# Two layers of gated cross attention on one core: held contexts, expert biases inside the expert products, gate picks on GpSimd, new orders

## The chip, the cores and the metric

The kernel runs on one NeuronCore of a Trainium2 chip. The metric is the device time in microseconds. Engines are named TensorE (PE in the rows; PEld is its weight load), VectorE (DVE), ScalarE (ACT), GpSimd (POOL) and SyncE (SP, which here only issues DMAs).

## The reference

There are 32 independent batches, each with x of 112 x 256 and a context of 375 x 192, in float32. Four updates follow each other:

```
x = x + tanh(g_xattn[0]) * (softmax(q k^T / 8) v) Wo^T + bo, 4 heads, q from layernorm(x), k and v from the context
x = x + tanh(g_ffn[0])   * layernorm(x) (W + up_aux lora_up lora_down down_aux)^T + b
x = x + tanh(g_xattn[1]) * softmax(q k^T) v             one head of 256, biases on q, k, v
x = x + tanh(g_ffn[1])   * (self attention of 16 heads + experts)
```

(the gate of the first line also covers bo, that of the second b). The experts: a softmax over 8 gate logits, of which the two largest are kept as weights; the output is the sum over e of weight[e] * (x W_experts[e] + b_experts[e]). layernorm has no scale or shift.

## The kernel before, in words

Every engine runs its own written program. The batches go through a software pipeline: in iteration i, each body handles batch a = i (layer 0's keys and values), b = i-1 (layer 0's scores), c = i-2 (layer 0's end, its linear layer and the queries of layer 1), d = i-3 (layer 1's attention, the projections of the last layer) and e = i-4 (16-head attention, experts, store). There are 32 + 4 iterations; the first five and the last four are unrolled, the others are one loop. What an engine does in which order is the list of calls in its `body`; there is no scheduler. Engines meet by semaphores: a `Chain` counts the steps of one batch, and `after(step, batch)` is the value to wait for.

Nearly all products are split: an operand is a float16 high half and a float16 low half, and a product is three matmuls (high x high, high x low, low x high). ScalarE writes the high half (`hi`), VectorE the low half (`lo`).

PSUM is one tile `quad` of four banks and the banks B, C, D and E. `quad` is used in turn by the keys and values (`project_k`, `project_v`), the scores of layer 0 (`scores0`, `scores0_T`) and those of the 16 heads (`scores2`, `scores2_T`). A score product is made twice: once for its row maximum (VectorE reduces it, `max0`, `max1`, `max2`, and TensorE transposes the maximum, `max0_T`, ...), and once transposed, with the maximum subtracted. Bank E holds two experts at a time: `experts(j)` makes 6 matmuls of 512 columns, `weigh_experts(j)` (ScalarE) scales them by the weights cgS into `part`, and `add_experts(j)` (GpSimd) adds them to `acc`.

The experts' bias is a product of its own. VectorE picks the two weights (`gate_pick`, `gate_combine`, `gate_weights`, `gate_scaled`), TensorE transposes them (`combine_T`), VectorE copies them as a high and a low half (`combine_copy`, `combine_lo`), TensorE multiplies them with the biases (`expert_bias`), and VectorE starts the sum with it (`start_sum`: acc = bias + x3). GpSimd's first `add_experts` and TensorE's `max2_T` wait for that sum.

GpSimd also makes the layernorms' 1/deviation (`rstd`, two small operations), which VectorE's `normalise` waits for, and one half of the context (`ctxT_hi`). Layer 1 needs the context's halves two iterations after layer 0: SyncE copies them from `kvA` to `kvB` and from there to `kc0`, `kcA`, `kcB`, `kcm`.

## Time and profile before

| | |
|---|---|
| median of 3 runs | 924.86 us (920.3 to 925.35) |
| the profiled execution | 923.47 us, its span 921.5 us |
| mean granted TensorE clock | 0.977 of full speed |
| busy, share of the span | PE 846.2 us (92%), DVE 785.2 us (85%), ACT 563.2 us (61%), POOL 392.7 us (43%) |
| matmuls | 11764 |
| DMA | 61.82 MB, mean 67 GB/s |

The span runs from the first to the last instruction. Matmuls are pipelined, and the end of one is modelled, so one row's length overlaps the next; the time that a matmul takes from TensorE is the distance from its start to the next start. A mean of a group is of single instructions. `project_k` is the mark by which iterations are told apart here: for batch 17 it starts at 449.76 us, for batch 18 at 476.22 us.

### The profile page before, as it was taken

Reading aid. Unit: us, or ns where it says so; the run is one execution under the profiler, and the core shown is the slowest. Engines: PE = TensorE matmul, PEld = TensorE weight load, DVE = VectorE, ACT = ScalarE, POOL = GpSimd, SP = SyncE. Lnnn points to the kernel's source line nnn. Section 1 sums busy time; section 2 is a strip of 40 time slices with the busy share of each in tenths; the row PEclk is TensorE's granted clock in tenths of the full one; section 3 lists DMA queues with packets and bytes.
Section 4 is the critical chain, followed back from the end, with each engine's and each line's share of the span. In section 5 each row is a group of like instructions: output and inputs, shape, how many; then the busy total and the mean of one; then the engine's idle time right before and its main releaser. Section 6 shows DMA issues by size and latency. Waiting matters only on the chain. (4 is left out here: it accounts for less than half of the span.)

```text
span 921.5 us, 34388 instructions
## 1 busy us (share of the span) xinstructions
PE 846.2 (92%) x11764; PEld 666.0 (72%) x11764; DVE 785.2 (85%) x1910; ACT 563.2 (61%) x1230; POOL 392.7 (43%) x603
## 2 busy tenths in 40 slices
PE   4678999999999999999999999999999999999876
PEld 2467777778777777787777778777777787777654
DVE  3588989989998989899899998998999889888654
ACT  2444666666666666666666666666666666666443
POOL 3311545433455453344554433445544334454433
PEclk9789999999999999999999999999999999999987
DMA  7311222121112211212222122122221211111100
GB/s 257 114 61 57 66 79 66 59 73 61 58 61 75 75 62 62 68 57 63 64 75 74 52 73 63 53 70 66 75 70 54 75 60 56 61 59 56 39 6 6
DMA packets 41285, 61.82 MB, mean 67 GB/s; under 512 B 6158, under 2 KB 28036, under 8 KB 41128
## 3 DMA queue, kind: packets, MB, share of 16 engines
q1 hardware_dynamic: 41256, 61.43, 20.9%
q8 instruction: 18, 0.29, 0.1%
q14 instruction: 11, 0.09, 0.0%
HBM read 37.77 MB, written 3.67 MB: 45 GB/s over the span
## 5 line engine op out<-in xcount | busy, mean ns | idle before, releaser
L1317 POOL TENSOR_TENSOR acc<-part,acc 112x256 f32<-112x256 f32 x256 | 212.4, 830 | 298.9 <-DVE acc L1163 275.3
L820 ACT ACTIVATE part<-bankE,cgS 112x256 f32<-112x256 f32 x256 | 107.2, 473 | 3.0 <-PE bankE L329 2.3
L1266 POOL TENSOR_SCALAR ln_ve<-ln_mv 112x1 f32<-112x1 f32 x128 | 33.9, 265 | 174.5 <-DVE ln_mv L967 173.2
L329 PE MATMUL bankE<-wexs_hi,xT_hi 128*112 128x512 f16 x256 | 99.3, 388 | 3.4 <-ACT part L820 3.4
L1270 POOL TENSOR_TENSOR ln_rs<-ln_ve,cst 112x1 f32<-112x1 f32 x128 | 94.5, 738 | 10.7
L329 PE MATMUL bankE<-wexs_hi,xT_lo 128*112 128x512 f16 x256 | 97.7, 382 | 0.0
L329 PE MATMUL bankE<-wexs_lo,xT_hi 128*112 128x512 f16 x256 | 97.7, 382 | 0.0
L1067 DVE TENSOR_TENSOR p_lo<-p2T,p_hi 112x896 f16<-112x896 f32 x64 | 67.6, 1094 | 9.6 <-ACT p_hi L811 9.6
L1130 DVE TENSOR_REDUCE mx<-quad 112x8 f32<-112x896 f32 x64 | 69.6, 1088 | 1.0
L740 ACT ACTIVATE p0T<-quad 125x896 f32<-125x896 f32 x64 | 46.2, 722 | 38.6 <-PE quad L445 38.6
L973 DVE TENSOR_SCALAR xn<-x,ln_mv,ln_rs 112x256 f32<-112x256 f32 x96 | 54.9, 572 | 5.9 <-POOL ln_rs L1270 2.0
L803 ACT ACTIVATE p2T<-quad 112x896 f32<-112x896 f32 x64 | 55.2, 914 | 5.9 <-PE quad L579 2.7
L1001 DVE TENSOR_TENSOR p_lo<-p0T,p_hi 125x896 f16<-125x896 f32 x64 | 54.1, 845 | 5.1 <-ACT p_hi L748 5.1
L811 ACT ACTIVATE p_hi<-p2T 112x896 f16<-112x896 f32 x64 | 57.0, 944 | 0.0
L988 DVE TENSOR_REDUCE mx<-quad 112x2 f32<-112x750 f32 x64 | 56.7, 925 | 0.3 <-PE quad L423 0.2
L329 PE MATMUL quad<-kvA,linw_hi 128*128 128x375 f16 x192 | 53.2, 333 | 2.7 <-ACT p0T L740 1.5
L329 PE MATMUL quad<-linw_hi,kvA 128*125 128x256 f16 x288 | 54.8, 274 | 0.0
L748 ACT ACTIVATE p_hi<-p0T 125x896 f16<-125x896 f32 x64 | 48.9, 764 | 4.6
L956 DVE SCALAR_TENSOR_TENSOR kvA<-ctf,kvA 128x375 f16<-128x375 f32 x32 | 33.0, 1030 | 20.4 <-POOL kvA L1308 20.4
L329 PEld LDWEIGHTS bankE<-wexs_hi,xT_lo 128*112 128x112 f16 x256 | 33.5, 131 | 22.4 <-issue 0.6
L329 PE MATMUL bankC<-p1T,ctn 125*128 125x112 f32 x384 | 48.1, 275 | 0.4 <-ACT p1T L767 0.4
L329 PEld LDWEIGHTS bankE<-wexs_hi,xT_hi 128*112 128x112 f16 x256 | 33.4, 131 | 20.8 <-ACT part L820 4.5
(239 smaller groups left out, 3275.5 us busy)
## 6 DMA issues: line engine op xcount, KB each, us to landing
ctf<-in_ctx_T SPq DMA_DIRECT2D x32, 375.0 KB, 3.1
ctn<-in_ctx_n SPq DMA_DIRECT2D x32, 375.0 KB
kvB<-kvA SPq DMA_DIRECT2D x32, 281.2 KB, 2.4
kc<-kvB SPq DMA_DIRECT2D x32, 187.5 KB
xin<-in_x SPq DMA_DIRECT2D x32, 112.0 KB, 2.0
x<-in_x SPq DMA_DIRECT2D x32, 112.0 KB, 2.1
out_x<-xout SPq DMA_DIRECT2D x32, 112.0 KB, 1.9
wex<-in_w_exp SPq DMA_DIRECT2D x1, 2048.0 KB, 9.9
```

The costliest lines, as they stand in the source:

```text
L329: last = mm(o, w, m, start=(n == 0), stop=(n == len(terms) - 1))
L748: act.activation(p0_hi[:, :, cs, :, 0:LQ].rearrange("p r c j q -> p r (c j) q"), p0T[:, :, cs].rearrange("p r c j q -> p r (c j) q"), ACT. ...
L803: act.activation(p2T[:, 2 * g:2 * g + 2].rearrange("p n i q -> p n (i q)"), quad[0:LQ, 2 * g:2 * g + 2, 0:4 * LQ], ACT.Exp, scale=HD1 ** - ...
L811: act.activation(p2_hi[:, 2 * g:2 * g + 2, :, 0:LQ], p2T[:, 2 * g:2 * g + 2], ACT.Copy).then_inc(st2[g].sem, 1)
L820: act.activation(part[:, e, :], bankE[0:LQ, n * D:(n + 1) * D], ACT.Identity, scale=cgS[:, e:e + 1])\
L973: ts(xn[n][:], src[:], ln_mv[n][:, 0:1], ln_rs[n][:], ALU.subtract, ALU.mult).then_inc(ln[n].sem, 1)
L988: dve.tensor_reduce(mx0[:].rearrange("p (r j) -> p r j", r=2)[:, :, g], quad[0:LQ, 2 * g:2 * g + 2, 0:LK], AX.X, ALU.max).then_inc(sh0[g]. ...
L1001: tt(p0_lo[:, :, cs, :, 0:LQ].rearrange("p r c j q -> p r (c j) q"), p0T[:, :, cs].rearrange("p r c j q -> p r (c j) q"), p0_hi[:, :, cs, ...
L1067: tt(p2_lo[:, 2 * g:2 * g + 2, :, 0:LQ].rearrange("p n i q -> p (n i) q"), p2T[:, 2 * g:2 * g + 2].rearrange("p n i q -> p (n i) q"), p2_h ...
L1130: dve.tensor_reduce(mx2[:].rearrange("p (n w) -> p n w", n=4)[:, 2 * g:2 * g + 2, 0:4], quad[0:LQ, 2 * g:2 * g + 2, 0:4 * LQ].rearrange("p ...
L1270: pool.tensor_tensor(ln_rs[n][:], ln_ve[n][:], minus_half, ALU.pow).then_inc(ln[n].sem, 1)
L1317: pool.tensor_tensor(acc[:], part[:, 2 * j + n, :], acc[:], ALU.add).then_inc(moe_sum[j].sem, 1)
```

## The change

- **Contexts.** `kvB` is gone. SyncE writes `kvA` to a DRAM tensor `hold` of 32 slots (`hold_context`) and loads the layer-1 tiles from there (`fetch_held`); the wait of `copy_A_to_B` for the previous copy out of `kvB` is gone.
- **Biases.** Each `experts(j)` gets a seventh matmul of 512 columns, 16 (in two rows, a high and a low half) times the biases of its two experts. `combine_T`, `expert_bias`, `combine_copy`, `combine_lo`, `start_sum` and `acc` go. The biases are packed once, by ScalarE (`bex_half`) and VectorE (`bias_experts(j)`).
- **Picks.** `gate_pick`, `gate_combine` and `gate_weights` run on GpSimd, the last one writes cgS directly (the gate's scale is in `ths`); `gate_scaled` goes. The reciprocal stays on VectorE (`gate_recip`).
- **Sums.** `add_experts` adds in `part` itself: expert k's slot becomes the sum of 0..k and x3. `finish` reads the last slot, in a sixth stage f, one iteration later; `weigh_experts` waits slot by slot.
- **Loads.** The weights of `lin` come in four DMAs, the constants, the keys' start values and the LoRA matrices in another order; the high halves of WK and WV are separate.
- **Orders.** All bodies have a new order, and loops start at another place of the iteration. Six iterations are unrolled ahead, five behind.

```
-STAGES = 5
+STAGES = 6
-PEEL = 5
+PEEL = 6
-        kvA, kvB = sb("kvA", [P, 3, LK], F16), sb("kvB", [P, 3, LK], F16)
+        kvA = sb("kvA", [P, 3, LK], F16)
+        hold = nc.dram_tensor("hold", [NB, P, 3, LK], F16, kind="Internal").ap()
...
-            def copy_B_to_C(b):
+            def fetch_held(b):
-                sp.wait_ge(copyAB.sem, copyAB.after("c", b))
+                sp.wait_ge(held.sem, held.after("c", b))
                 if past(b - 1):
                     sp.wait_ge(st1.sem, st1.after("ps", b - 1))
-                sp.dma_start(kc0[:], kvB[:, 0:2, :]).then_inc(copyBC.sem, DMA)
+                sp.dma_start(kc0[:], hold[b, :, 0:2, :]).then_inc(fetched.sem, DMA)
...
-            def copy_A_to_B(a):
+            def hold_context(a):
                 sp.wait_ge(ctT[0].sem, ctT[0].after("lo", a))
                 sp.wait_ge(ctT[1].sem, ctT[1].after("lo", a))
-                if past(a - 1):
-                    sp.wait_ge(copyBC.sem, copyBC.after("m", a - 1))
-                sp.dma_start(kvB[:], kvA[:]).then_inc(copyAB.sem, DMA)
+                sp.dma_start(hold[a], kvA[:]).then_inc(held.sem, DMA)
...
             def max2_T(d):
                 pe.wait_ge(sh2.sem, sh2.after("max_b", d))
-                pe.wait_ge(acc_s.sem, acc_s.after("sum", d))
+                pe.wait_ge(qk_s.sem, qk_s.after("klo", d))
...
             def experts(j, d):
-                    wex_lo[:, c, cols].rearrange("p e n -> p (e n)"))]).then_inc(moe[j].sem, 1)
+                    wex_lo[:, c, cols].rearrange("p e n -> p (e n)"))]
+                    + [(ones16, bex[:, 2 * j * D:2 * (j + 1) * D])]).then_inc(moe[j].sem, 1)
...
+            def gate_pick(d):
+                pool.wait_ge(gate_s.sem, gate_s.after("indexf", d))
...
+                pool.tensor_scalar(pick0[:], iota, topf[:, 0:1], top[:, 0:1], ALU.is_equal, ALU.mult).then_inc(gate_s.sem, 1)
+                pool.tensor_scalar(pick1[:], iota, topf[:, 1:2], top[:, 1:2], ALU.is_equal, ALU.mult).then_inc(gate_s.sem, 1)
...
+            def gate_weights(d):
+                pool.wait_ge(gate_s.sem, gate_s.after("comb", d))
+                pool.wait_ge(rs_s.sem, rs_s.after("recip", d))
...
+                pool.tensor_scalar(cgS[:], comb[:], rsg[:], ths[0:LQ, 0:1], ALU.mult, ALU.mult).then_inc(gate_s.sem, 1)
...
-                    pool.tensor_tensor(acc[:], part[:, 2 * j + n, :], acc[:], ALU.add).then_inc(moe_sum[j].sem, 1)
+                    k = 2 * j + n
+                    pool.tensor_tensor(part[:, k, :], part[:, k, :], part[:, k - 1, :] if k else x3[:], ALU.add).then_inc(moe_sum[j].sem, 1)
...
+            load_ctx_T(0)
+            sp.dma_start(lin[:, WK], w_lin[:, WK]).then_inc(wk_in, DMA)
             sp.dma_start(gate_in[:], gates).then_inc(gates_in, DMA)
-            load_ctx_T(0)
-            sp.dma_start(lin[:, WK:WV + 1], w_lin[:, WK:WV + 1]).then_inc(kv_in, DMA)
+            sp.dma_start(lin[:, WV], w_lin[:, WV]).then_inc(wv_in, DMA)
+            load_x(0)
...
                 if A: project_k(a)
                 if DD: norm_T(3, d, bankD, pv2, "norm", d - 1)
+                if A: project_v(a)
                 if C: norm_T(2, c, bankC, f0_s, "x2", c)
-                if A: project_v(a)
                 if DD: project_vg(d)
...
                 if EE: exp2(0, e)
-                if EE: exp2(1, e)
                 if B: hi(qs, "ps", b, q_hi[:], cols(bankB, KD, LQ), 1 / SW, st0[1], "ps", b - 1)
+                if EE: exp2(1, e)
```

The last two pieces are lines of TensorE's and of ScalarE's `body`.

Three places of the new orders, in the loop. First TensorE around the sums of layer 1 (bankC<-p1T,ctn is `sums1`; cgb holds the weights to be transposed, bex16 the biases). Before:

```order
L329 MATMUL bankB<-stack,c16 112x256
L609 ISA
L610 REGISTER_ALU
L611 MATMUL bankD<-cst,cgb 128x112
L510 ISA
L329 MATMUL bankC<-p1T,ctn 128x112 x6
L616 ISA
L617 MATMUL bankD<-bex16,cT 112x256
L329 MATMUL bankE<-wexs_hi,xT3_hi 112x512
L329 MATMUL bankE<-wexs_lo,xT3_hi 112x512
```

Now:

```order
L333 MATMUL bankC<-m1h,kcm 125x112
L553 ISA
L555 ISA
L565 MATMUL quad<-k2_hi,q2_hi 112x112 x16
L402 ISA
L404 ISA
L406 MATMUL bankB<-cst,xn0 128x112 x2
L516 ISA
L333 MATMUL bankC<-p1T,ctn 128x112 x6
L596 ISA
```

The transpose of the weights and the bias product are gone; `scores2` and the transpose of `normalise(0)` stand between `scores1_T` and `sums1` where `project_o` and the weights' transpose stood. The bias is the last row of each group of bankE (`bankE<-bex,c16 112x512`, not in this piece).

Second VectorE, from the low halves of the 16 heads' probabilities (p2_lo) to the low half of the normalised x3 (xT3_lo), which `project_vg` waits for. Before:

```order
L1028 SCALAR_TENSOR_TENSOR x2<-bankC,x1 112x256
L956 SCALAR_TENSOR_TENSOR kvA<-ctf,kvs 128x375
L962 BN_STATS ln2_st<-x2 112x6
L967 BN_AGGR ln2_mv<-ln2_st 112x2
L970 REGISTER_ALU
L973 TENSOR_SCALAR xn3<-x3,ln3_mv,ln3_rs 112x256
L1137 RECIPROCAL rec2<-bankD 112x16
L1144 TENSOR_TENSOR o2<-bankD,rec2 112x256
L973 TENSOR_SCALAR xn2<-x2,ln2_mv,ln2_rs 112x256
L997 ISA
L1001 TENSOR_TENSOR p0_lo<-p0T,p0_hi 125x2x4x112
L956 SCALAR_TENSOR_TENSOR xT3_lo<-bankD,xT3_hi 128x224
```

Now (the two p2_lo stand right ahead):

```order
L980 SCALAR_TENSOR_TENSOR kvA<-ctf,kvA 128x375
L980 SCALAR_TENSOR_TENSOR kvA<-ctf,kvs 128x375
L1052 SCALAR_TENSOR_TENSOR x2<-bankC,x1 112x256
L986 BN_STATS ln2_st<-x2 112x6
L991 BN_AGGR ln2_mv<-ln2_st 112x2
L1140 RECIPROCAL rec2<-bankD 112x16
L1147 TENSOR_TENSOR o2<-bankD,rec2 112x256
L997 TENSOR_SCALAR xn2<-x2,ln2_mv,ln2_rs 112x256
L1021 ISA
L1025 TENSOR_TENSOR p0_lo<-p0T,p0_hi 125x2x2x112
L980 SCALAR_TENSOR_TENSOR xT3_lo<-bankD,xT3_hi 128x224
L1025 TENSOR_TENSOR p0_lo<-p0T,p0_hi 125x2x4x112
```

The first half of the context (kvA<-ctf,kvA) stood ahead of `max0` before and is in this stretch now, `normalise(3)` has gone out of it, ahead of p2_lo, and the shorter one of the two p0_lo stands ahead of xT3_lo instead of the longer one.

Third GpSimd, the end of its iteration (ln_ve, ln_rs: `rstd`). Before:

```order
L1270 TENSOR_TENSOR ln3_rs<-ln3_ve,cst 112x1
L1317 TENSOR_TENSOR acc<-part,acc 112x256 x2
L1266 TENSOR_SCALAR ln2_ve<-ln2_mv 112x1
L1270 TENSOR_TENSOR ln2_rs<-ln2_ve,cst 112x1
L1323 ISA
L1324 TENSOR_TENSOR xout<-o2,acc 112x256
L1264 ISA
L1266 TENSOR_SCALAR ln0_ve<-ln0_mv 112x1
L1267 REGISTER_ALU
L1270 TENSOR_TENSOR ln0_rs<-ln0_ve,cst 112x1
```

Now:

```order
L1252 REGISTER_ALU
L1255 TENSOR_TENSOR ln0_rs<-ln0_ve,cst 112x1
L1288 ISA
L1290 ISA
L1292 TENSOR_SCALAR pick0<-cst,topf,top 112x8
L1293 TENSOR_SCALAR pick1<-cst,topf,top 112x8
L1296 REGISTER_ALU
L1298 REGISTER_ALU
L1299 TENSOR_TENSOR comb<-pick0,pick1 112x8
L1302 REGISTER_ALU
L1309 TENSOR_SCALAR cgS<-comb,rsg,ths 112x8
L1329 TENSOR_TENSOR part<-part 112x256 x2
```

Four small operations of the gate now stand between the last `rstd` and the sums of the experts; the first of these rows of `part` is `add_experts(2, e)`, and `add_experts(0, d)` and `add_experts(3, e)` follow it.

## Rows read from the trace of the kernel before

**Rows 1.** Stretches: from:to, length; busy us (instructions) of each engine; TensorE clock, DMA share, GB/s

```profile
78.13:104.46 26.33, 25.32 (x368) 20.35 (x368) 23.80 (x59) 17.58 (x39) 12.03 (x16) 1.00 0.17 58
...
158.70:820.30 661.60, 640.30 (x9182) 507.23 (x9179) 601.26 (x1476) 432.02 (x951) 294.80 (x450) 1.00 0.21 66
...
820.30:921.50 101.20, 81.05 (x1037) 62.87 (x1033) 64.89 (x169) 48.78 (x114) 40.35 (x55) 0.89 0.09 27
...
449.76:476.22 26.46, 25.63 (x374) 20.30 (x371) 24.06 (x60) 17.29 (x39) 11.80 (x18) 1.00 0.21 66
```

**Rows 2.** TensorE in time: start, length, operation, idle before, in one steady iteration

```profile
468.68 0.38 PE L329 MATMUL bankE<-wexs_lo,xT_hi 128*112 128x512 f16 x1
468.89 0.38 PE L329 MATMUL bankE<-wexs_hi,xT_lo 128*112 128x512 f16 x1
469.49 0.53 PE L423 MATMUL quad<-k_hi,q_hi 64*112 64x375 f16 x4 [0.22 <-ACT q_hi L711]
...
471.40 0.38 PE L329 MATMUL bankE<-wexs_hi,xT_lo 128*112 128x512 f16 x1
472.29 0.29 PE L431 MATMUL bankB<-cst,mx 112*128 112x112 f32 x1 [0.51 <-issue]
```

**Rows 3.** Waits of 449.76 to 476.22: who waits for whom, us in total, times, longest

```profile
PEld bankB L431 <- DVE mx L988: 0.9, 1, 0.9
...
PEld quad L423 <- ACT p2T L803: 0.7, 1, 0.7
...
PEld bankC L400 <- DVE xn L973: 0.3, 1, 0.3
```

**Rows 4.** TensorE in time, the same iteration, around the experts' bias

```profile
461.97 0.26 PE L611 MATMUL bankD<-cst,cgb 112*128 112x112 f32 x1
462.07 1.50 PE L329 MATMUL bankC<-p1T,ctn 125*128 125x112 f32 x12
...
463.41 0.27 PE L617 MATMUL bankD<-bex,cT 128*112 128x256 f16 x1
463.52 0.38 PE L329 MATMUL bankE<-wexs_hi,xT_hi 128*112 128x512 f16 x1
```

**Rows 5.** VectorE groups by form: operation, shapes, count, busy us, mean ns, idle before

```profile
L1163 DVE TENSOR_TENSOR acc<-bankD,x 112x256 f32<-112x256 f32 x32 | 13.6, 425 | 1.1
...
L1117 DVE TENSOR_SCALAR cgb<-comb,rsg,th 112x24 f32<-112x24 f32 x32 | 9.2, 287 | 0.1
...
L1103 DVE TENSOR_SCALAR pick<-cst,topf,top 112x8 f32<-112x8 f32 x32 | 9.1, 283 | 0.0
...
L1156 DVE SCALAR_TENSOR_TENSOR cT<-bankD,cT 8x112 f16<-8x112 f32 x32 | 8.6, 267 | 1.1
...
L1124 DVE TENSOR_SCALAR cgS<-cgb 112x8 f32<-112x8 f32 x32 | 5.2, 162 | 0.0
```

**Rows 6.** GpSimd groups by form

```profile
L1317 POOL TENSOR_TENSOR acc<-part,acc 112x256 f32<-112x256 f32 x256 | 212.4, 830 | 298.9 <-DVE acc L1163 275.3 <-ACT part L820 6.8 <-POOL acc L1317 4.4
...
L1266 POOL TENSOR_SCALAR ln_ve<-ln_mv 112x1 f32<-112x1 f32 x128 | 33.9, 265 | 174.5 <-DVE ln_mv L967 173.2
```

**Rows 7.** VectorE in time, the same iteration, after the scores of layer 0

```profile
470.42 1.77 DVE L988 TENSOR_REDUCE mx<-quad 112x2 f32<-112x750 f32 x2
472.11 0.38 DVE L956 SCALAR_TENSOR_TENSOR xT_lo<-bankC,xT_hi 128x224 f16<-128x224 f32 x1
```

**Rows 8.** VectorE groups by form: the two lower halves of the context

```profile
L956 DVE SCALAR_TENSOR_TENSOR kvA<-ctf,kvA 128x375 f16<-128x375 f32 x32 | 33.0, 1030 | 20.4 <-POOL kvA L1308 20.4
...
L956 DVE SCALAR_TENSOR_TENSOR kvA<-ctf,kvs 128x375 f16<-128x375 f32 x32 | 22.9, 714 | 4.7 <-ACT kvs L721 4.7
```

**Rows 9.** ScalarE in time, at the program's start

```profile
12.00 1.04 ACT L669 ACTIVATE linw_hi<-lin 128x1024 f16<-128x1024 f32 x1
13.07 0.51 ACT L721 ACTIVATE kvs<-ctf 64x375 f16<-64x375 f32 x1
```

**Rows 10.** TensorE in time, at the program's start

```profile
12.15 1.09 PE L343 MATMUL bankE<-t,luT 4*50 4x256 f32 x2 [0.46 <-ACT t L682]
14.38 0.78 PE L329 MATMUL quad<-kvA,linw_hi 128*128 128x375 f16 x2 [1.14 <-DVE kvA L956]
```

More of the change, by code:

```diff
@@ L177, in flamingo_kernel @@
         bqkvg_s = chain("bqkvg_s", "scaled half packed")
[L178 to L181 removed]
+        bex_s = [chain(f"bex{j}_s", "scaled half packed") for j in range(NG)]
+        bex_zero = sem("bex_zero")
+        wk_s, wv_s, wqo_s, wf_s, wqk_s, wvg_s = (chain(n + "_s", "hi lo") for n in ("wk", "wv0", "wqo", "wf", "wqk", "wvg"))
         wex_s = [chain(f"wex{j}_s", "hi lo") for j in range(NG)]
@@ L192, in flamingo_kernel @@
         xTs = [chain(f"xT{n}s", "ps hi lo") for n in range(4)]
-        acc_s = chain("acc_s", "sum")
         qs = chain("qs", "ps hi lo")
@@ L209, in flamingo_kernel @@
         vg_s = chain("vg_s", "ps v lo max negmax exp")
-        gate_s = chain("gate_s", "top index indexf pick0 pick1 comb recip bias scaled")
+        gate_s = chain("gate_s", "top index indexf pick0 pick1 comb scaled")
+        rs_s = chain("rs_s", "recip")
         sh2 = chain("sh2", "ps max_a max_b")
@@ L381, in project_v @@
             def project_v(a):
+                if first(a):
+                    pe.wait_ge(wv_s.sem, wv_s.after("lo", 0))
                 if past(a - 1):
@@ L1158, in start_sum, with body @@
-            def start_sum(d):
-                dve.wait_ge(cb_s.sem, cb_s.after("ps", d))
-                dve.wait_ge(o1_s.sem, o1_s.after("x3", d))
-                if past(d - 1):
-                    dve.wait_ge(fin.sem, fin.after("sum", d - 1))
-                tt(acc[:], bankD[0:LQ, 0:D], x3[:], ALU.add).then_inc(acc_s.sem, 1)
             def xT_lo(n, b, bank, free, fstep):
                 lo(xTs[n], b, xT[n][1][:], cols(bank, KD, LQ), SX, xT[n][0][:], free, fstep, b - 1)
-            def body(a, b, c, d, e):
-                A, B, C, DD, EE = (v is not None for v in (a, b, c, d, e))
-                if EE: combine_lo(e)
+            def body(a, b, c, d, e, f):
+                A, B, C, DD, EE, FF = (v is not None for v in (a, b, c, d, e, f))
+                if B: mean_var(0, b)
+                if EE: gate_neg(e)
+                if C: norm0(c)
+                if DD: lo(qps, d, qp_lo[:], cols(bankC, KD, LQ), 1 / SW, qp_hi[:], st1, "ps", d - 1)
+                if EE: gate_max(e)
+                if EE: gate_index(e)
+                if B: normalise(0, xin, b)
+                if A: wk_lo(a)
+                if A: wv_lo(a)
+                if C: out0_lo(c)
+                if B: lora_add(b)
+                if EE: gate_indexf(e)
+                if DD: max1(d)
+                if EE: gate_recip(e)
+                if B: keys_lo(b)
+                if B: values_lo(b)
+                if C: residual(wo_s, "x1", c, x1, bankB, x0, f0_s, "x2", 1)
+                if EE: q2_lower(e)
+                if EE: k2_lower(e)
+                if C: stats(1, x1, wo_s, "x1", c)
+                if EE: max2(0, e)
@@ L1310, in add_experts @@
             def add_experts(j, d):
-                before = acc_s if j == 0 else moe_sum[j - 1]
-                pool.wait_ge(before.sem, before.after("sum" if j == 0 else "odd", d))
+                if j == 0:
+                    pool.wait_ge(o1_s.sem, o1_s.after("x3", d))
+                else:
+                    pool.wait_ge(moe_sum[j - 1].sem, moe_sum[j - 1].after("odd", d))
                 for n, step in enumerate(("even", "odd")):
@@ L1413 @@
     l1v[DK, D] = 1.0
-    b_exp = np.zeros((T, D), np.float32)
-    for j in range(0, 96, 32):
-        b_exp[j:j + E] = np.asarray(L1_ffn_b_experts)
     arrays = {
```

411 lines of the change are left out of this document (196 added, 215 removed).

## Prediction

> **What bounds the kernel now.** I read the table of stretches first, then one steady iteration in it, then TensorE's timeline and the list of waits of that iteration, then VectorE's groups. From 78.13 to 820.30 us `project_k` starts 28 times at nearly equal distance; the table shows the first of these iterations with 26.33 us, and 25 of them in 661.6 us, 26.46 us each, at the full clock (1.00) [rows 1]. So 742 of 921.5 us are one repeated iteration, and the question is what its 26.46 us consist of. In the one from 449.76 to 476.22 TensorE is busy 25.63 us and VectorE 24.06 us; ScalarE (17.3) and GpSimd (11.8) have room, and so has DMA, at 0.21 of its time [rows 1]. Two engines are close to the bound, and they take turns in one chain.
>
> TensorE's busy time hides waits, since a row's end overlaps the next start. I therefore use start-to-start distances. A 512-column matmul takes 0.21 us (468.68 to 468.89). From the last matmul of `experts(2)` to `scores0` it is 0.60 (468.89 to 469.49): 0.39 of waiting. From the last matmul of `experts(3)` to `max0_T` it is 0.89 (471.40 to 472.29): 0.68 of waiting [rows 2]. The waits name the other side: L431 waits for VectorE's reductions mx, L423 for ScalarE's exponentials p2T, L400 for VectorE's xn, 0.3 us [rows 3]. Smaller handovers (`scores2`, `project_q`, `ffn0`, `scores0_T`) I put together at 0.4, an estimate of 0.1 each. That makes about 1.8 us of waiting (0.68 + 0.39 + 0.3 + 0.4), and 24.7 us of TensorE's own work, in 26.46.
>
> VectorE reaches the first `max0` late: `scores0` starts at 469.49, the reduction at 470.42, and it never waits in between; the two take until 472.11, 1.69 us [rows 2, 7]. So the largest of TensorE's waits is one for a VectorE that is behind, not for the length of the chain.
>
> **The change, part by part.** *Biases, TensorE.* Added: 4 matmuls of 512 columns, 4 x 0.215 = 0.86 us per iteration. Removed: the transpose of the weights, 0.10 (461.97 to 462.07), and the bias product, 0.11 (463.41 to 463.52) [rows 4]. Net +0.65 us, on the engine that is nearest to the bound, uncovered: TensorE's own work goes from 24.7 to 25.3. Over 28 iterations that alone is +18.2 us.
>
> *Biases and picks, VectorE.* Removed: the start of the sum 0.43, the weights 0.29, two picks of 0.28, two copies of cT of 0.27, cgS 0.16 and the sum comb, which I take as long as cgS [rows 5]: 2.15 us. Its 24.06 become 21.9. Nothing of that shows in the time unless TensorE waited for it, and it can give back at most the waits that TensorE has.
>
> *Picks, GpSimd.* Four small operations in a chain. The nearest row is 0.27 us (one column), the far one 0.83 (256 columns, two inputs) [rows 6]: 1.1 to 3.3 us, and I take 1.4, since they have 8 columns. They stand between `gate_indexf` and `weigh_experts(0)`. VectorE issues `gate_indexf` ahead of `max1`, and `weigh_experts(0)` follows `exp1`, after `experts(0)` (1.5 us), `project_o` and `scores1_T`: some 3 us later. At 1.4 this is covered; at 3.3 it would delay `weigh_experts(0)` by 0.4 us.
>
> *Sums.* `max2_T` loses its wait for the start of the sum, 0.43 us of VectorE behind the second `max2`. `add_experts(2)` and `(3)` run later, but only `finish` and the slots of `part` wait for them, most of an iteration later. I cost it at nothing; the cover is GpSimd's 14.7 idle us per iteration [rows 1].
>
> *Contexts.* As many DMAs and bytes per iteration. `hold_context` stands where `copy_A_to_B` stood, behind `fetch_held`, without its wait for the previous copy. Its consumer `ctxT_hi` is behind the next iteration's `rstd(3)`. I take 0. If a write to DRAM lands over 2 us later than the copy did, GpSimd stops there, with `rstd(2)` behind it, and `normalise(2)` and `norm_T(2)` behind that.
>
> *Orders.* Here is where the waits go or come back, so I walked through the new order with start-to-start times.
> First `max0_T`. VectorE no longer has the 1 us of kvA ahead of it [rows 8]. I let the first reduction start 0.4 us after `scores0`, the second end at 2.1. TensorE comes to `max0_T` 2.12 us after `scores0` now (469.49 to 471.61), with the bias matmul 2.33 [rows 2, 7]. The 0.68 go.
> Second `scores0`. `experts(2)` is 0.215 longer and q_hi is no longer last: of 0.39 I leave 0.1.
> Third `sums1`, new: after `scores1_T` only `scores2` and a transpose remain as cover for the exponential of layer 1, where there were `project_o` and a transpose: 0.2.
> Fourth VectorE's stretch from `max0` to xT3_lo. It holds both kvA halves now, 1.0 and 0.7 us [rows 8]. `project_k` waits for them right behind p2_lo: 0.3. `project_vg` has only the short p0_lo ahead of it: 0.
> The small ones I leave at 0.2 in sum.
> Total of the waits: 0.8 instead of 1.8. The iteration: 26.46 + 0.65 - 1.8 + 0.8 = 26.1 us. VectorE, at 21.9 of 26.1, permits that.
>
> *Start.* `project_k(0)` starts at 14.38; it waited for kvs, which ScalarE wrote at 13.07, behind the weights' high half of 12.00, and the second LoRA matmul ran at 12.15 [rows 9, 10]. Now kvs is early and `project_k` can follow the LoRA matmul, at about 13.2: -1.2. But four DMAs more stand ahead of the last LoRA matrix, which TensorE waits for first. I take -0.6, with +2 as the other end.
>
> *End.* The last 101.2 us [rows 1] hold four iterations with experts: 4 x 0.65 = +2.6 at most, and 0.43 + 2 x 0.27 = 0.97 less of VectorE's work ahead of `max2_T` in each [rows 5], -3.9 at most. I take 0.
>
> **Sum.** 28 x (26.1 - 26.46) = -10.1, start -0.6, end 0: -10.7. The profiled execution took 923.47 us (2 us around its span): 912.8. The median of the runs is 1.4 above that execution, so 914 (912.8 + 1.4, rounded).
>
> **A rule against it.** The normalised xn and the copies into kvA are VectorE operations beside GpSimd's. The lower half with kvA as its input takes 1.03 us, and 0.71 for the same shape with kvs; in the first, GpSimd adds experts beside it [rows 8, 6]. The Trainium skill, SBUF — State Buffer, Who interferes with whom, says that GpSimd and VectorE share a pair of ports as an exclusive lock: a VectorE operation with two SBUF inputs, or in a two-port mode, and a GpSimd one block each other fully. By that rule the trace's 0.3 us are such a block, and each operation moved to GpSimd can cost VectorE its own length; the sum by it would be 4 x 0.27 = 1.1 us of VectorE's gain of 2.15 given back. What it does here is the last rival.
>
> **Rivals.**
> 1. *The waits stay, the matmuls are paid for.* TensorE's waits are the length of chains through ScalarE and PSUM, not a late VectorE; then 26.46 + 0.65 = 27.1, 28 x 0.65 = +18: 942, slower. For: the second largest wait is one for ScalarE, and TensorE is busy 25.63 of 26.46 [rows 1, 3]. Against: the reduction starts 0.93 us after `scores0` with VectorE never idle. It decides from the point where less than 0.65 us of waiting goes.
> 2. *The waits move.* The order puts `ctxT_lo` right ahead of `project_k`, and `rstd(2)` and `normalise(2)` ahead of xT3_lo; with 0.35 us more of waiting than I count, the iteration is 26.45: 924, no change. For: VectorE's stretch from `max0` to xT3_lo is some 9 to 10 us without a gap, as long as TensorE's work beside it.
> 3. *TensorE runs without a wait.* 25.3 + 0.2 = 25.5: 28 x -0.96 = -27: 897. Against: four handovers per iteration go through ScalarE in any order.
> 4. *GpSimd is late* with cgS (3.3 us above) or by the lock: +0.4 per iteration, +11 on the forecast: 925.
> 5. *The DRAM write is late*: 1 us per iteration on `rstd(2)`, +28 on the forecast: 942. Against: DMA is 0.21 busy, and `ctxT_hi` stands behind five other GpSimd operations of its iteration.
>
> **How the numbers follow.** The forecast 0.45 (iterations of 25.7 to 26.3, 903 to 920), rival 1 0.14, rival 2 0.22, rival 3 0.11, rival 4 0.05, rival 5 0.03. About 0.5% (4.6 us) is what a measurement of this kernel can tell from no change. Faster by more than that: 0.42 of the forecast, rival 3, and 0.07 of rivals 2 and 4: 0.60. Slower: rivals 1 and 5, and 0.04 of rivals 2 and 4: 0.21. Within: 0.19. The range goes from 895 to 935; rivals 1 and 5 (0.17) and little else lie outside.
>
> **What would show it.** In the profile after: `project_k` to `project_k` 26.1 us; TensorE's busy time in it 0.6 higher; VectorE's busy time 2.1 lower and with real gaps; L431's successor without a wait for mx, and small waits at `sums1` and `project_k`; cgS written by GpSimd before `exp1` ends; `hold` landing in under 4 us. If the iteration is 27 us, or the wait for mx stays, the walk through the order was wrong; if VectorE's busy time falls by much less than 2.1, the lock is at work.

## The result, and the profile after

The changed kernel takes 901.32 us (median of 4 runs, 900.34 to 902.24), the kernel before 924.85: a ratio of 0.9755, 95% interval 0.9727 to 0.9783. The forecast was 914. The sign was right, the size was not: 23.5 us less, where 10.7 were forecast.

The stretches of the profiled execution (span 899.3 us), in the columns of [rows 1]: the iteration that begins at `project_k(3)` (still ahead of the loop), a steady iteration, and the end, which is all that follows the last `project_k`.

```profile
78.00:103.70 25.70, 25.51 (x370) 20.82 (x371) 22.29 (x51) 17.35 (x40) 9.12 (x16) 1.00 0.18 50
...
415.05:441.03 25.98, 25.80 (x376) 20.78 (x373) 20.74 (x52) 16.89 (x39) 11.42 (x22) 1.00 0.23 67
...
804.70:899.30 94.60, 77.67 (x1046) 60.12 (x1043) 55.50 (x138) 48.17 (x113) 42.31 (x75) 0.95 0.10 29
```

The iteration takes 25.98 us instead of 26.46; VectorE is busy for 20.74 of it instead of 24.06; the end takes 94.6 us instead of 101.2 [rows 1]. Over the span that is 22.2 us less: 0.1 in the start (both kernels start `project_k(3)` at 78), 15.5 in the 28 iterations (742.2 to 726.7), 6.6 in the end. Of the 15.5, 2.8 lie in the first two iterations: in the kernel before, the first pass through the loop takes 27.77 us.

TensorE in time, the places of [rows 2] in the iteration from 415.05:

```profile
434.33 0.38 PE L333 MATMUL bankE<-bex,c 128*112 128x512 f16 x1
434.66 0.53 PE L429 MATMUL quad<-k_hi,q_hi 64*112 64x375 f16 x4
435.12 0.41 PE L406 MATMUL bankC<-cst,xn 112*128 112x112 f32 x2
435.64 0.42 PE L333 MATMUL bankE<-wexs_hi,xT_hi 128*112 128x512 f16 x1
...
436.98 0.38 PE L333 MATMUL bankE<-bex,c 128*112 128x512 f16 x1
437.20 0.26 PE L437 MATMUL bankB<-cst,mx 112*128 112x112 f32 x1
```

From the last matmul of `experts(3)` to `max0_T` it is 0.22 us, a matmul's own length, where it was 0.89; to `scores0` it is 0.33, where it was 0.60. One handover is longer: from the transposes of xn to the first matmul of `experts(3)` it is 0.52 (435.12 to 435.64), where it was 0.33 (469.95 to 470.28 in the iteration of [rows 2]). VectorE beside it, then GpSimd's new operations:

```profile
434.14 0.17 DVE L991 BATCH_NORM_AGGREGATE ln_mv<-ln_st 112x2 f32<-112x6 f32 x1
435.07 1.79 DVE L1012 TENSOR_REDUCE mx<-quad 112x2 f32<-112x750 f32 x2 [0.76 <-PE quad L429]
...
439.39 0.54 DVE L980 SCALAR_TENSOR_TENSOR kvA<-ctf,kvA 128x375 f16<-128x375 f32 x1
439.85 0.54 DVE L980 SCALAR_TENSOR_TENSOR kvA<-ctf,kvs 128x375 f16<-128x375 f32 x1
```

```profile
424.34 0.41 POOL L1292 TENSOR_SCALAR pick<-cst,topf,top 112x8 f32<-112x8 f32 x1 [1.80 <-DVE topf L1121]
424.73 0.40 POOL L1293 TENSOR_SCALAR pick<-cst,topf,top 112x8 f32<-112x8 f32 x1
425.30 0.20 POOL L1299 TENSOR_TENSOR comb<-pick 112x8 f32<-112x8 f32 x1 [0.16 <-POOL pick L1293]
425.70 0.35 POOL L1309 TENSOR_SCALAR cgS<-comb,rsg,ths 112x8 f32<-112x8 f32 x1 [0.20 <-POOL comb L1299]
```

VectorE now waits 0.76 us for the scores and begins 0.41 after `scores0` (it was 0.93). The four picks take 1.71 us from first start to end (forecast 1.4). All of this looked like the forecast's mechanism. The runs show that most of it has another cause.

### The profile page after: what moved, and what is told of

Same layout as the page of the kernel before. It is cut to its first block and busy times, and to the rows that moved or that the text cites. A ratio compares the mean times of both kernels' runs of the same rounds, so it can differ in the third digit from the quotient of the medians.

```text
span 899.3 us, 34510 instructions
## 1 busy us (share of the span) xinstructions
PE 849.3 (94%) x11828; PEld 678.3 (75%) x11828; DVE 685.0 (76%) x1657; ACT 556.3 (62%) x1240; POOL 384.4 (43%) x731
## 5 line engine op out<-in xcount | busy, mean ns | idle before, releaser
L1251 POOL TENSOR_SCALAR ln_ve<-ln_mv 112x1 f32<-112x1 f32 x128 | 30.9, 242 | 370.5 <-DVE ln_mv L991 370.4
L1329 POOL TENSOR_TENSOR part<-part 112x256 f32<-112x256 f32 x224 | 163.0, 733 | 13.6 <-POOL part L1329 4.1
L1255 POOL TENSOR_TENSOR ln_rs<-ln_ve,cst 112x1 f32<-112x1 f32 x128 | 72.7, 568 | 10.7
L1133 DVE TENSOR_REDUCE mx<-quad 112x8 f32<-112x896 f32 x64 | 66.2, 1075 | 1.7 <-PE quad L565 1.7
L812 ACT ACTIVATE p2T<-quad 112x896 f32<-112x896 f32 x64 | 58.5, 919 | 10.2 <-PE quad L585 10.2
L1025 DVE TENSOR_TENSOR p_lo<-p0T,p_hi 125x448 f16<-125x448 f32 x64 | 54.4, 850 | 1.5 <-ACT p_hi L757 1.4
L997 DVE TENSOR_SCALAR xn<-x,ln_mv,ln_rs 112x256 f32<-112x256 f32 x96 | 39.9, 416 | 15.8 <-POOL ln_rs L1255 15.8
L333 PE MATMUL bankC<-p1T,ctn 125*128 125x112 f32 x384 | 51.1, 283 | 0.5 <-ACT p1T L776 0.5
L333 PEld LDWEIGHTS bankE<-wexs_hi,xT_lo 128*112 128x112 f16 x256 | 33.3, 130 | 22.2 <-issue 0.2
L333 PEld LDWEIGHTS bankC<-p1T,ctn 125*128 125x128 f32 x384 | 45.5, 192 | 4.8 <-ACT p1T L776 1.1
L333 PE MATMUL bankE<-bex,c 128*112 128x512 f16 x128 | 48.5, 379 | 0.0
```

The lines of the kernel that those rows point to most:

```text
L333: last = mm(o, w, m, start=(n == 0), stop=(n == len(terms) - 1))
L812: act.activation(p2T[:, 2 * g:2 * g + 2].rearrange("p n i q -> p n (i q)"), quad[0:LQ, 2 * g:2 * g + 2, 0:4 * LQ], ACT.Exp, scale=HD1 ** - ...
L997: ts(xn[n][:], src[:], ln_mv[n][:, 0:1], ln_rs[n][:], ALU.subtract, ALU.mult).then_inc(ln[n].sem, 1)
L1025: tt(p0_lo[:, :, cs, :, 0:LQ].rearrange("p r c j q -> p r (c j) q"), p0T[:, :, cs].rearrange("p r c j q -> p r (c j) q"), p0_hi[:, :, cs, ...
L1133: dve.tensor_reduce(mx2[:].rearrange("p (n w) -> p n w", n=4)[:, 2 * g:2 * g + 2, 0:4], quad[0:LQ, 2 * g:2 * g + 2, 0:4 * LQ].rearrange("p ...
L1255: pool.tensor_tensor(ln_rs[n][:], ln_ve[n][:], minus_half, ALU.pow).then_inc(ln[n].sem, 1)
```

## The experiments

Each kernel was run beside the kernel before, whose median lay between 922.8 and 924.5. "Iteration" is the distance of `project_k` to `project_k` in the steady part. The edits are shown in part, with "..." where more of them is left out; the words behind a # are explanations of mine, not of the code.

For the start and the end one must know how far equal code differs. before_hold and before_hold_unrl (both below) run the same code up to `project_k(3)` and reach it at 76.1 and 79.8 us. The changed kernel and unrolled (below) issue the same operations behind the last `project_k` and take 94.6 and 97.3 us for them. A difference of one profile with another in the start or the end that is not larger than that shows nothing.

### First: which part of the change

**old_orders**, all but the new orders:

```
-STAGES = 6
+STAGES = 5
...
-                if C: out0_T(c)
-                if A: lora_1(a)
-                if DD: scores1(d)
                 if EE: experts(0, e)
                 if DD: max1_T(d)
+                if C: out0_T(c)
+                if EE: scores2(e, b, c)
...
```

> Everything of the change but the orders: the bodies of all engines are in the order of before (five stages, five iterations unrolled), with the bias chain gone, the seventh matmul in, the picks on GpSimd at the end of its iteration, the contexts held in DRAM and the new loads. Theory A (relief): the gain comes from the 2.15 us of VectorE's work and the bias chain that are gone, the orders add little; an iteration takes 26.0 to 26.2 us, the end behind the last project_k 95 to 97 us, in all about 907. Theory B (orders): the relief alone is eaten by the added matmuls (+0.65 us), an iteration takes 26.4 to 27.1 us, and in all 920 to 940; then the end stays above 99 us.

906.82 us (905.01 to 908.16), iteration 25.94. The time is that of theory A and the iteration just below its 26.0, but the end (99.9) is that of theory B. With the context held in DRAM, the new orders give nothing in the steady state. The 5.5 us between the two kernels lie in the start (`project_k(3)` at 80.8 instead of 78.0, no more than equal code differs) and in the end (99.9 instead of 94.6).

**no_bias_mm**, the changed kernel without the 7th matmul:

```
-    + [(ones16, bex[:, 2 * j * D:2 * (j + 1) * D])]).then_inc(moe[j].sem, 1)
+    ).then_inc(moe[j].sem, 1)
```

> The changed kernel without the seventh matmul of each expert pair: the experts' bias is left out of the result. If TensorE's own work is the bound of an iteration, it falls by the full 4 x 0.215 = 0.86 us, from 25.98 to 25.1, and the time by 25 to 28 us, to about 875. If the chains through ScalarE and VectorE bound it, TensorE waits where it worked, and less than half of that shows: above 888.

894.0 us (893.22 to 894.95), iteration 25.67: 0.86 us less work for TensorE shortens it by 0.31. So not all of its work is on the path. (This kernel leaves the experts' bias out of its result.)

**picks_dve**, the picks back on VectorE behind `gate_recip`:

```
-                if DD: gate_pick(d)      # and gate_combine, gate_weights, on GpSimd
+                if EE: gate_pick(e)      # and the other two, on VectorE
```

> The changed kernel with the two picks, their sum and the weights on VectorE again, behind the gate's reciprocal (0.28 + 0.28 + 0.16 + 0.16 = 0.9 us per iteration for VectorE). Theory A (VectorE has slack at 20.7 of 26 us busy): within 3 us of the changed kernel's 901. Theory B (VectorE's chain from max1 over the keys' and values' low halves to max2 has no slack, as the walk through the order said): TensorE waits for values_lo and max2, 0.4 to 0.9 us more per iteration, 912 to 926.

938.88 us (938.33 to 940.05), iteration 27.23, beyond both expectations. At this place VectorE has no slack: the wait ahead of `scores2` grows by about 1 us.

**lo0_early**, the changed kernel with `ctxT_lo(0)` ahead of `max0` again:

```
-                if A: ctxT_lo(0, a)      # behind probs2_lo(1)
+                if A: ctxT_lo(0, a)      # ahead of max0(0)
```

> The changed kernel with one call moved: VectorE makes the context's first lower half (ctxT_lo(0)) ahead of max0 again, as before the change. If the wait of max0_T came from that, it returns: 0.3 to 0.7 us per iteration at max0_T, less up to 0.2 won at project_k, so +0.1 to +0.5 us, 904 to 915. If VectorE now has room ahead of scores0, nothing changes: 900 to 903.

977.96 us (972.42 to 980.5), iteration 28 and more: outside both expectations. The waits of 400 to 530 name the reason: who waits for whom, us in total, times, longest.

```profile
PEld bankB L437 <- DVE mx L1012: 10.2, 5, 2.0
...
DVE kvA L980 <- POOL kvA L1317: 8.8, 5, 1.8
```

`ctxT_lo(0)` waits for `ctxT_hi` on GpSimd, and everything behind it on VectorE waits too. That was the first sign of the cause found below.

### Second: the picks, the copy, and mixed orders

**old_picks_dve**, old_orders with the picks at their old places on VectorE:

```
-                if DD: gate_pick(d)      # on GpSimd
+                if DD: gate_pick(d)      # on VectorE, behind values_lo
```

> The kernel of old_orders (all of the change but the new orders), with the two picks, their sum and the weights cgS on VectorE as before, at their old places between max1 and max2. Against old_orders (906.8, iteration 25.94) only VectorE gets longer, by about 1 us per iteration (two picks of 0.28, a sum and cgS of 0.16 each), to 23.5; against the kernel before (924.5, 26.46) only the bias chain is gone and its matmuls added. Theory A: the relief of VectorE as a whole decides, whatever part of it is cut; the iteration goes back by 1/2.15 of the 0.52 us, to about 26.2, 912 to 917. Rival B: what counted was the bias chain, whose sum stood directly ahead of max2_T; the picks have slack: 905 to 909. Rival C: the picks stand in the first half of the iteration, where VectorE has no slack (in picks_dve they cost more than their length): the whole microsecond comes back, 26.8 to 27: 930 or more.

907.01 us (904.86 to 908.45), iteration 25.93, as old_orders: rival B's number. VectorE's extra microsecond costs nothing here.

**old_dve_pool** and **old_all_but_pe**, the changed kernel with the bodies of two or three engines in the old order:

```
-            def body(a, b, c, d, e, f):  # VectorE, GpSimd (and ScalarE): new
+            def body(a, b, c, d, e, f):  # the old one, f unused
```

> The changed kernel with the old order on VectorE and GpSimd; TensorE, ScalarE and SyncE in the new order. old_orders takes 906.8 and the changed kernel 901.3, with the same iteration (25.94 and 25.98): 2.8 us lie in the start, 5.3 in the end. Theory A: both are TensorE's order (what it has to do while it waits in the drain): this kernel stays at 900 to 903. Rival B: they are VectorE's and GpSimd's orders (the last experts' sums and finish ahead, or the gate's statistics): 905 to 908. Rival C: old and new orders side by side disturb the steady iteration, which was arranged for one set: 910 or more.

> The changed kernel with the old order on ScalarE, VectorE and GpSimd; only TensorE and SyncE in the new order. Theory A, TensorE's order makes the start and the end shorter: 900 to 903. Rival B, ScalarE's order does it (with old_dve_pool at 901 and this at 906). Rival C, a mixture disturbs the steady iteration: 910 or more.

1124.31 and 1122.64 us, iterations of 31.7 to 34.5. Rival C in both, and far beyond its number. An order is one thing over all engines; by mixing, the start's and the end's gain can't be put down to one engine, and this stays open.

**kvB_back**, the changed kernel with the copy in SBUF:

```
...
-                sp.dma_start(hold[a], kvA[:]).then_inc(held.sem, DMA)
+                if past(a - 1):
+                    sp.wait_ge(fetched.sem, fetched.after("m", a - 1))
+                sp.dma_start(kvB[:], kvA[:]).then_inc(held.sem, DMA)
```

> The changed kernel with the second context buffer in SBUF again in place of the array in DRAM: hold_context waits for the previous fetch, then copies kvA to kvB; fetch_held reads kvB. All else is as in the changed kernel. Theory A: holding in DRAM moves nothing, since the copy is fetched long before: 900 to 903. Rival B: the wait for the previous fetch keeps kvA busy, and ctxT_hi on GpSimd is late as in the long pass of the kernel before (27.77 us): 0.3 us or more per iteration, 909 or more. Rival C: the copy within SBUF is quicker to land than the write to DRAM and lets kvA go earlier: 896 to 899.

901.34 us (900.34 to 906.1), iteration 25.98. I read this as "the hold is worth nothing". It is true only of the new orders: with them the copy in SBUF costs nothing, with the old ones it costs 18 us (old_kvB, below).

### Third: loops and the end

**unrolled** and **before_unrolled**, every iteration written out:

```
-PEEL = 6
+PEEL = 32
...
-            with eng.Fori(PEEL, NB) as i:
-                body(i, i - 1, i - 2, i - 3, i - 4, i - 5)
...
```

> The changed kernel with every iteration written out: no loop on any engine, all addresses and waits constant. In the changed kernel, old_orders and kvB_back the first iteration whose project_k lies in the written-out part takes 25.6 us and each iteration of the loop 25.94 to 25.98, with the same work; in the loop TensorE's gaps are longer ahead of out0_T, norm_T(0) and scores0_T (0.13, 0.08, 0.13 us). Theory A: these 0.35 us are the price of the loop (its branch and the register arithmetic on the engines that TensorE waits for): 26 x 0.35 = 9 us less, 891 to 894. Rival B: the first iterations are quicker because part of the work of the later ones is not there yet: 899 to 903. Rival C: the longer program has to be fetched, and engines stop for it: 905 or more.

> The kernel before with every iteration written out. Its iterations in the loop take 26.46 us, the first one in the loop 27.77 (ctxT_hi on GpSimd waits for the copy of kvA to kvB), the one ahead of the loop 26.33. Theory A, as for unrolled: the loop costs it 0.1 to 0.35 us per iteration and the 1.3 us of that long pass: 4 to 10 us, 914 to 920; then the gain of the change without loops is 22 to 27 us. Rival B: nothing of it is the loop: 922 to 926. Rival C: fetching the program costs: 930 or more.

unrolled: 895.36 us (893.97 to 896.37), ratio to the kernel before 0.9686 (0.966 to 0.9711); iteration 25.61. Theory A's iteration came, 0.37 us less each; the end took 97.3, 2.7 more with the same operations, so the total missed its number. before_unrolled: 951.75 us (947.58 to 954.3), outside all expectations: iterations drift from 26.4 to 31.2 and fall back. Its waits from 386 to 439, two iterations:

```profile
PEld bankB L427 <- DVE mx L984: 6.2, 2, 3.3
POOL kvA L1304 <- DMA kvB<-kvA: 6.2, 2, 3.3
DVE kvA L952 <- POOL kvA L1304: 5.7, 2, 3.1
```

A chain can be read in it: the copy, `ctxT_hi`, `ctxT_lo(0)`, `max0`, `max0_T`.

**fill_end**, the changed kernel with matmuls into an unused bank while TensorE waits in the end:

```
+                if late: fill(6 if DD else 8)
                 if EE: values2(e)
...
```

> The changed kernel with matmuls of 512 columns added in the last two bodies with experts, into a bank that nothing reads any more: 6 and 8 ahead of values2, 4 ahead of norm_T(3), 3 ahead of the last scores2, each time about as long as TensorE waits there now (1.7, 2.1, 1.1 and 0.9 us). Nothing that counts is computed otherwise. The granted clock in the last two stretches is 0.94 and 0.85 now. Theory A: the low clock of the end is a result of these gaps, and TensorE's length at the low clock is on the path: the clock stays at 1.00 for longer, and the end gets 1 to 3 us shorter: 898 to 900. Rival B: the chain through the other engines sets the end: 900 to 903, whatever the clock. Rival C: the matmuls are longer than the waits: 903 to 906.

900.66 us (899.93 to 904.96): by the median, rival B. But the six executions differ. Four took 899.9 to 900.7 us at a mean granted clock of 0.985 (the changed kernel: 0.981), and two took 904.5 and 905.0 at 0.976 and 0.980. The profiled one is the 904.5. In its last stretch (880 to 902.7) the clock was 0.95 instead of 0.85, but in the one from 831 to 857 it was 0.87 instead of 0.98, and its end takes 97.3 us, not 94.6. The ends of fill_end and unrolled:

```profile
805.40:902.70 97.30, 83.75 (x1067) 64.33 (x1063) 55.55 (x138) 48.10 (x113) 42.28 (x75) 0.93 0.09 28
...
796.30:893.60 97.30, 80.15 (x1046) 62.54 (x1042) 55.42 (x138) 48.13 (x113) 42.23 (x75) 0.91 0.10 29
```

So this run does not show that the clock is without effect on the end. The ends of the other runs speak for one. With the new orders it takes 94.6 us at a clock of 0.95 (the changed kernel and kvB_back) and 97.3 at 0.91 (unrolled); with the old ones 97.9 and 98.5 at 0.91 (sum_wait and chain_back, below) and 99.9 at 0.89 (old_orders). Of the 5.3 us between 99.9 and 94.6 the orders are then worth about 1, at the same clock, and the rest goes with the clock: an estimate from these few executions. Whether the clock makes the end longer, or a longer end with more waiting of TensorE has the lower clock, was not tested.

### Fourth: what made VectorE late at `max0`

**chain_back** and **sum_back**: old_picks_dve with stand-ins on VectorE that nobody waits for, for all three operations of the bias chain or for `start_sum` alone.

```
...
                 if EE: max2(1, e)
+                if EE: stand_in(2, e)
...
```

> old_picks_dve (907.0 us, iteration 25.93, VectorE busy 22.5 of it) with three VectorE operations added that read constants and that nobody waits for, where the old chain had its own: one like combine_copy behind max2(0), one like combine_lo at the head of the body, one like start_sum behind max2(1); together 0.8 to 1.0 us per iteration. TensorE's work is unchanged. Theory A: VectorE's length decides, being behind at max0: most of the 0.53 us per iteration comes back, 26.3 to 26.8 and 917 to 930. Rival B: the chain's handovers between TensorE, ScalarE and VectorE were the cost (transpose, cT, product), VectorE's length was free: 905 to 910. Rival C: VectorE slips below its point of no slack as in before_unrolled, and GpSimd's sums come late with it: 935 or more.

> old_picks_dve with only the stand-in for start_sum (320 columns, about 0.4 us) behind max2(1), between the second reduction and the residual of layer 0. Theory A: at this place VectorE has some slack for 0.4 us: in the kernel with old orders the picks of 1 us cost nothing either: 906 to 909. Theory A': each part of VectorE's length counts once it is behind: half of what chain_back brings back, 911 to 918. Rival B as for chain_back: 905 to 909 for both.

906.72 us (906.02 to 907.49) and 906.29 us (905.61 to 907.49), iteration 25.93 in both. chain_back's stretch from 400 to 530:

```profile
400.00:530.00 130.00, 129.24 (x1848) 103.68 (x1847) 119.28 (x291) 85.65 (x190) 63.71 (x90) 1.00 0.24 67
```

VectorE is busy for 119.28 of 130 us, 23.8 per iteration, nearly as in the kernel before (24.06), and nothing is lost. Theory A, the forecast's relief of VectorE, falls, as long as the context is held in DRAM, as it is here. Rival B, the handovers of the bias chain, was left.

**before_x3_sum** and **sum_wait**: GpSimd's wait for `start_sum`, 8.3 us in each iteration before, taken out of the kernel before, and put into sum_back.

```
...
-                before = acc_s if j == 0 else moe_sum[j - 1]
+                if j == 0:
+                    pool.wait_ge(o1_s.sem, o1_s.after("x3", d))
...
```

> The kernel before with one dependence changed: GpSimd's sum of the experts begins from x3 (ready long before) instead of acc. The whole bias chain is still issued (weights, transpose, cT, product, start_sum into a tile of its own that nobody reads), so the experts' bias is missing in the result; the orders, the copy of the contexts in SBUF and the 6 matmuls per pair of experts are as before. Theory D: the cost of the chain was GpSimd standing for it: GpSimd adds the first experts about 2.5 us earlier, rstd(1) and ctxT_hi come earlier, VectorE reaches max0 in time and TensorE's wait of 0.7 at max0_T goes: iteration 25.6 to 25.8, the long pass of 27.77 goes too: 898 to 908. Theory A (VectorE's length, which is unchanged): 922 to 926. Theory B (the chain's handovers on TensorE, unchanged): 922 to 926.

> sum_back (906.3 us, iteration 25.93) with one wait added: add_experts(0) on GpSimd waits for the stand-in behind max2(1), as it waited for start_sum before. Nothing else is changed, and no operation added. Theory D: rstd(1), ctxT_hi and the sums come about 2.5 us later, VectorE gets late at max0, and TensorE waits at max0_T: the iteration goes to 26.3 to 26.9 (the matmuls of the bias are in it too), 917 to 933. Theory B: 905 to 909.

921.24 us (918.59 to 924.0), iteration 26.45; and 904.95 us (904.55 to 905.25), iteration 25.93, though GpSimd now waits 7.5 us for the stand-in in each. Theory D falls in both directions. (before_x3_sum leaves the experts' bias out of its result.)

Then I laid the iterations of the kernel before and of old_picks_dve side by side. They are alike up to `scores0` (19.74 us behind `project_k` in both) and part at `max0`. The kernel before, in one iteration, SyncE's queue, GpSimd, and VectorE in time:

```profile
461.34 0.50 SPq L264 DMA_DIRECT2D kc<-kvB  x1
...
463.92 0.83 SPq L268 DMA_DIRECT2D kcm<-kvB  x1
465.86 0.49 SPq L275 DMA_DIRECT2D kvB<-kvA  x1
```

```profile
466.88 0.57 POOL L1270 TENSOR_TENSOR ln_rs<-ln_ve,cst 112x1 f32<-112x1 f32 x1
468.46 0.52 POOL L1308 TENSOR_SCALAR kvA<-ctf 128x375 f16<-128x375 f32 x1 [1.01 <-DMA kvB<-kvA]
```

```profile
469.11 1.09 DVE L956 SCALAR_TENSOR_TENSOR kvA<-ctf,kvA 128x375 f16<-128x375 f32 x1 [0.61 <-POOL kvA L1308]
470.12 0.38 DVE L956 SCALAR_TENSOR_TENSOR q_lo<-bankB,q_hi 128x224 f16<-128x224 f32 x1
```

The copy is issued 1.1 us after the last fetch has been issued (464.75), and the kernel makes `copy_A_to_B` wait for the fetch to land. `ctxT_hi` waits for the copy. VectorE waits 0.61 us for that, and its `ctxT_lo(0)` is slow (1.09) beside GpSimd's adds. Then q_lo, and only then `max0`, at 470.42 [rows 7].

**before_hold** and **old_kvB**: the hold in DRAM alone put into the kernel before, and alone taken out of old_picks_dve.

```
...
-                if past(a - 1):
-                    sp.wait_ge(copyBC.sem, copyBC.after("m", a - 1))
-                sp.dma_start(kvB[:], kvA[:]).then_inc(copyAB.sem, DMA)
+                sp.dma_start(hold[a], kvA[:]).then_inc(copyAB.sem, DMA)
```

> The kernel before with one part of the change alone: kvA is written to an array in DRAM and fetched from there, without the wait for the previous fetch. Bias chain, picks, orders and loads are as before. Theory E: the copy to kvB, issued only when the fetch from kvB has landed, kept ctxT_hi on GpSimd, and with it ctxT_lo(0), q_lo and max0 on VectorE, 0.5 us late per iteration. The write to DRAM goes out 1.1 us earlier and lands about 0.3 us later: the iteration goes to 25.8 to 26.0, the long pass of 27.77 to about 26: 905 to 911. Rival F: the gain needs the bias chain's relief as well, since VectorE is at 24 of 26.46: 916 to 922. Rival A and the forecast (hold = 0): 922 to 926.

> old_picks_dve (907.0 us, iteration 25.93) with the copy in SBUF again (kvB, and the wait for its previous fetch). Theory E: max0 is late again by 0.5 us, plus the 7th matmul of experts(3) is no longer hidden: iteration 26.4 to 26.7, with a long pass, 918 to 928. Rival F: with the shorter VectorE the lateness is absorbed: 905 to 912.

before_hold: 905.78 us (905.13 to 908.96), ratio 0.9814 (0.9783 to 0.9846), iteration 25.97. old_kvB: 925.32 us (924.75 to 927.58), ratio 1.0016 (1.0001 to 1.003), iteration 26.61. Theory E in both (in old_kvB without a long first pass). before_hold, an iteration and the same operations on SyncE's queue, GpSimd and VectorE:

```profile
439.80:465.80 26.00, 25.66 (x375) 20.33 (x372) 24.02 (x60) 17.20 (x39) 11.57 (x18) 1.00 0.22 67
```

```profile
451.56 0.35 SPq L265 DMA_DIRECT2D kc<-hold  x1
...
453.91 0.30 SPq L269 DMA_DIRECT2D kcm<-hold  x1
454.44 0.38 SPq L274 DMA_DIRECT2D hold<-kvA  x1
```

```profile
456.97 0.57 POOL L1269 TENSOR_TENSOR ln_rs<-ln_ve,cst 112x1 f32<-112x1 f32 x1
457.63 0.52 POOL L1307 TENSOR_SCALAR kvA<-ctf 128x375 f16<-128x375 f32 x1
```

```profile
458.68 0.81 DVE L955 SCALAR_TENSOR_TENSOR kvA<-ctf,kvA 128x375 f16<-128x375 f32 x1
459.58 0.39 DVE L955 SCALAR_TENSOR_TENSOR q_lo<-bankB,q_hi 128x224 f16<-128x224 f32 x1
459.98 1.79 DVE L987 TENSOR_REDUCE mx<-quad 112x2 f32<-112x750 f32 x2
```

The write goes out 0.2 us after the last fetch has been issued (454.21), GpSimd doesn't wait, VectorE doesn't wait, and `max0` starts 0.40 us after `scores0` (459.58). VectorE's busy time is the 24 us of before, and the bias chain is still there, so rival B falls too.

The hold has two parts that no run takes apart. From the issue of the first fetch to that of the copy or write it is 4.52 us before (461.34 to 465.86) and 2.88 now (451.56 to 454.44). About 0.9 of these 1.6 us is the wait that is gone (the pause of 1.1 against 0.2); the rest is that the five fetches are issued faster from DRAM than from SBUF. Each part, 0.9 and 0.7 us, is longer than the 0.61 us for which VectorE stood, so either might be enough alone.

**before_hold_unrl**, before_hold written out:

```
-PEEL = 5
+PEEL = 32
...
-            with eng.Fori(PEEL, NB) as i:
-                body(i, i - 1, i - 2, i - 3, i - 4)
...
```

> before_hold (905.8) with every iteration written out. Theory E: the late copy is what made the written-out kernel before drift (iterations of 26.4 to 31, 951.8 us); without it the iterations are even and lose the loop's 0.3 us each: 896 to 900. Rival G: the drift comes from the old bias chain (GpSimd waiting for acc, 8.2 us at the longest): uneven iterations again, 915 or more. Rival H: neither gain nor drift, 903 to 908.

897.36 us (892.31 to 898.13), ratio 0.9701 (0.9656 to 0.9746), iterations even at 25.54, and 25.37 at three places: theory E. The drift of before_unrolled was the copy as well.

The lowest median is that of unrolled, 895.36 us, and the intervals of the ratio of unrolled and before_hold_unrl overlap. All executions of both lie below those of the changed kernel.

## Why the prediction was right in sign and wrong in size

The mechanism of the forecast was a VectorE with too much work, relieved. Two of its steps failed: the reading of VectorE's lateness, with the price of the contexts that follows from it, and the price of the end. The first had the cause wrong, the second most of the size. By its own steps:

- *Biases, TensorE, +0.65.* The matmuls and transposes came as counted, but the price did not: with the hold in place, the iteration is 25.97 with 6 matmuls and the chain (before_hold) and 25.93 with 7 and without it (old_picks_dve). Only 0.31 of the 0.86 us of added matmuls is on the path (no_bias_mm, new orders). The forecast charged the net 0.65 in full, 18 us over the loop.
- *Biases and picks, VectorE, -2.15.* Measured -3.3; the copies into kvA and xn<-xin have also become shorter (below). With the hold in place, VectorE's length was worth nothing in the steady iteration (chain_back, old_picks_dve). Without the hold it was not tested alone.
- *Picks, GpSimd.* 1.71 us, covered, as forecast.
- *Sums, 0.* Right as far as GpSimd's wait for `start_sum` goes (before_x3_sum, sum_wait).
- *"A VectorE that is behind", and contexts: "I take 0".* **The step whose mechanism failed.** VectorE never waited between `scores0` and `max0`, as the forecast says, but just ahead of `scores0` it had stood still for 0.61 us, waiting for `ctxT_hi`, and that for the copy. The forecast noted that the write goes "without its wait for the previous copy" and priced only a late landing. Alone in the kernel before, the hold gives 18.5 us (924.33 to 905.78), 14.9 of them in the iterations of the profiles (742.2 to 727.3). [rows 8] had the hint: 20.4 us of idle time ahead of the lower half, put down to GpSimd's kvA, 0.64 per iteration. I used that row for the 1030 ns alone. Beside the new orders the price of 0 comes out true (kvB_back), for a reason that the forecast did not give.
- *Orders, `max0_T`, -0.68.* The wait went. The forecast's way, no kvA ahead of `max0`, is a second one to the same gain: with the copy in SBUF the iteration is 26.61 in old_kvB (old orders, picks on VectorE) and 25.98 in kvB_back. So in the changed kernel the orders and the hold each cover for the other, and the gain can't be divided between them.
- *Orders, the other waits.* `scores0` kept 0.1, as forecast. The 0.5 at `sums1` and `project_k` did not come. Not forecast were 0.19 more ahead of `experts(3)`, and three gaps that the loop makes 0.34 longer in sum (last section). That 26.1 lies near the 25.98 is in part luck.
- *First iterations.* The forecast took all 28 alike. The long pass of 27.77 went, also with the hold alone (25.80).
- *Start, -0.6.* Measured -0.1, in its bounds, and less than equal code differs.
- *End, 0.* **The step whose size failed, and the largest single miss.** Measured -6.6, beyond its own bound of -3.9. The forecast counted matmuls and VectorE's work there and had no term for the clock, which was 0.89 in the end before and 0.95 after. 5.3 us of the 6.6 separate the changed kernel from old_orders; by the estimate under fill_end some 1 us belongs to the orders as such and the rest goes with the clock. Which engine's order does it, and why the clock stays up, is open; unrolled, with the same operations in the end, had 0.91 in it.

In numbers, from -10.7: the end -6.6, the first two iterations -2.1 (-2.8 for -0.7), the other 26 together -3.2 (0.48 for 0.36), the start +0.5: -22.1, the span's -22.2.

Of the rivals, none happened. *GpSimd is late by the lock* had the wrong sign here. The operation xn<-xin takes 0.81 us where GpSimd adds beside it (in the kernel before) and 0.40 where GpSimd stands still (before_x3_sum). In the new orders kvA's copies no longer lie beside those adds, and xn mostly not: the first copy of kvA goes from 1030 to 541 ns. The Trainium skill, SBUF — State Buffer, Who interferes with whom, calls this an exclusive lock of a shared pair of ports. The trace agrees in direction; beside an add of 0.73 us that began 0.05 earlier, kvA's copy took 0.55 longer (1.09 for 0.54), somewhat less than the 0.67 that a full block would add.

## What to carry to other kernels

Follow a late engine back through everything that stood ahead of it in its queue, idle time included: the cause here was a DMA upstream (copy, `ctxT_hi`, `ctxT_lo(0)`, `max0`), through engines whose busy time said nothing. Price every wait that a change removes, above all when you have already asked only whether its replacement is slow. And before you credit a gain to one part of a change, put that part alone into the old kernel: taking it out of the new one (kvB_back) showed nothing, because another part, the new orders, covered for it. Last, look how far equal code differs in the start and the end, and at the granted clock there, before a difference of one profile with another is put down to a part of the change.
